# Attention with Toeplitz bias: pieces of the maxima and additions of the outputs on GpSimd, outputs turned later, another order in the last steps

## What is computed

```
proj = layernorm(x) @ w_in.T                     # k, v, q: 16 heads of 8 features
bias[h, i, j] = sum_k amp * exp(-|sharp| * (offset - (i - j))**2)   # depends on i - j: Toeplitz
logits = q @ k.T / sqrt(8) + bias
out = softmax(logits) @ v
x = x + out
```

## Time and profile before

| | |
|---|---|
| profiled execution | 1109.1 us, its span 1107.4 us |
| other runs | 1102.92, 1107.15, 1109.07 us |
| PE busy | 957.4 us (86%) |
| DVE busy | 855.9 us (77%) |
| ACT busy | 677.8 us (61%) |
| POOL busy | 487.8 us (44%) |
| mean granted TensorE clock | 0.934 |

### The profile page before, as it was taken

The page is one execution under the profiler, slowest core; times in us unless marked ns, Lnnn a source line. Parts: engine busy times, 40 slices in busy tenths (PEclk is TensorE's granted clock), DMA queues, the critical chain, the costliest instruction groups (busy, mean ns, idle before and its releaser), DMA issues. The chain is left out here.

```text
span 1107.4 us, 21223 instructions
## 1 busy us (share of the span) xinstructions
PE 957.4 (86%) x7613; PEld 561.8 (51%) x7613; DVE 855.9 (77%) x2203; ACT 677.8 (61%) x1042; POOL 487.8 (44%) x454
## 2 busy tenths in 40 slices
PE   4899999999999999866899999783877359999998
PEld 2423333333333333315777888541666347778886
DVE  7689999999999999766897554586896787975553
ACT  5226665666666566654678888587333136788886
POOL 4400101110110010104689999615674027899997
PEclk9669999999999999998999999996998669999999
DMA  4840223141314310005466677200000045666973
GB/s 103 230 161 17 84 77 72 36 125 39 75 47 113 66 35 2 3 1 145 133 178 175 170 191 193 57 19 1 0 0 0 3 101 156 172 180 159 220 193 95
DMA packets 80613, 105.92 MB, mean 96 GB/s; under 512 B 18252, under 2 KB 41602, under 8 KB 80514
## 3 DMA queue, kind: packets, MB, share of 16 engines
q1 hardware_dynamic: 78631, 102.43, 35.7%
q10 hardware_dynamic: 1883, 2.21, 0.7%
HBM read 95.84 MB, written 8.52 MB: 94 GB/s over the span
## 5 line engine op out<-in xcount | busy, mean ns | idle before, releaser
L663 POOL TENSOR_TENSOR f_act_low<-f_act,f_act_high 128x512 fp32r<-128x512 f32 x272 | 353.1, 1314 | 154.4 <-ACT f_act_high L639 146.6
L1509 DVE CUSTOM_DVE_ANT_0 at_rows<-at_rows,at_table_max 128x512 f32<-128x512 f32 x512 | 340.8, 718 | 26.3 <-PE at_rows L1295 17.0
L1455 ACT ACTIVATE at_prob<-at_cols 128x1024 f32<-128x1024 f32 x256 | 248.1, 1021 | 174.3 <-PE at_cols L1336 174.3
L678 DVE SCALAR_TENSOR_TENSOR f_gated<-f_hid,f_cw 128x512 f32<-128x512 f32 x256 | 174.1, 687 | 115.8 <-ACT f_act L644 86.9
L644 ACT ACTIVATE f_act<-f_gated 128x512 f32<-128x512 f32 x272 | 172.1, 633 | 109.8 <-DVE f_gated L678 78.5
L639 ACT CAST f_act_high<-f_act 128x512 fp32r<-128x512 f32 x272 | 164.9, 607 | 0.0
L1295 PE MATMUL at_rows<-at_k_stack,at_q_stack 48*64 48x512 bf16 x1024 | 128.3, 413 | 16.9 <-DVE at_maxima L1509 15.2
L1348 PE MATMUL at_pv<-at_prob,at_v_stack 128*32 128x512 f32 x1024 | 136.7, 606 | 0.6 <-ACT at_prob L1455 0.6
L1336 PE MATMUL at_cols<-at_table_cols,flip_sum 64*64 64x512 f16 x2048 | 135.4, 380 | 0.0
L610 PE MATMUL f_acc<-f_act_high,wd_high 128*128 128x512 f32 x272 | 109.1, 401 | 9.1 <-POOL f_act_low L663 8.9
L1295 PEld LDWEIGHTS at_rows<-at_k_stack,at_q_stack 48*64 48x64 bf16 x1024 | 36.4, 107 | 146.1 <-DVE at_maxima L1509 124.7
(11 more groups left out here) (322 smaller groups left out, 1360.0 us busy)
## 6 DMA issues: line engine op xcount, KB each, us to landing
f_cw<-f_c_rows SPq DMA_DIRECT2D x256, 256.0 KB, 4.5
at_table_cols<-bias_rows SPq DMA_DIRECT2D x64, 124.0 KB, 4.4
at_table_max<-bias_rows SPq DMA_DIRECT2D x12, 480.0 KB, 4.7
at_q_stack<-q_parts SPq DMA_DIRECT2D x32, 96.0 KB, 2.6
at_k_stack<-k_parts SPq DMA_DIRECT2D x24, 96.0 KB, 3.4
at_raw_weights<-in_L_ffn_up_w_dram SPq DMA_DIRECT2D x8, 256.0 KB, 4.1
at_raw_weights<-in_L_ffn_down_w_dram SPq DMA_DIRECT2D x8, 256.0 KB, 5.7
at_table_max<-bias_rows ACTq DMA_DIRECT2D x4, 480.0 KB, 5.8
```

What stands on the lines that cost most here:

```text
L663: nc.gpsimd.tensor_tensor(act_l[:, n % PART_SLOTS, :], act[:, n % ACT_SLOTS, :], act_h[:, n % PART_SLOTS, :].bitcast(F32), ALU.subtract).t ...
L678: ins = nc.vector.scalar_tensor_tensor(out=gated[:, n % GATE_SLOTS, :], in0=hid[:, n % HID_SLOTS, :], scalar=0.0, in1=cw[:, k % C_SLOTS, u ...
L1455: act(prob[:, S % 2, 2 * hp:2 * hp + 2, :], s2[:, hp, :, :], ACT.Exp).then_inc(exp_done, 1)
L1509: nc.vector.tensor_tensor_reduce(out=slot, in0=slot, in1=t_max[:, 2 * p.hp + j, c:c + BANK][:, ::-1], scale=1.0, scalar=-3.0e38, op0=ALU.a ...
```

## The change

GpSimd cuts the maxima into pieces: VectorE keeps the reduction over the two halves, and four chained GpSimd instructions make the pieces of the positive maximum (`cut_maxima`); the sign moves to the constant, now -1.0. The maxima are double-buffered by phase. GpSimd adds the normalised outputs to x for the first 12 of 16 phases (`add_rows`). In steps S%8 = 2 the outputs are turned behind the first rows pair instead of ahead of it, on TensorE, on VectorE and in the ring's order. The wait for the bias tables stands ahead of the scores. In the steps without rows pairs TensorE's order is scores 0, biases 0, maxima's turn, products of the step before, scores 1, biases 1.

```diff
+ADDED_ON_POOL = PHASES - 2 * BATCH
-TWO_ONES = struct.unpack("<f", struct.pack("<I", 0x3F803F80))[0]
+TWO_MINUS_ONES = struct.unpack("<f", struct.pack("<I", 0xBF80BF80))[0]
+def phase_cut_in(S):
+    n = [n for n in pairs_of_step(S) if n % PHASE_PAIRS == PHASE_PAIRS - 1]
+    return n[0] // PHASE_PAIRS if n else None
...
         for S in range(ALL_STEPS):
             pairs = pairs_of_step(S)
+            for n in pairs[:1]:
+                self.take(("pair", n), 2)
             if phase_out_in(S) is not None:
                 self.take(("out", phase_out_in(S)), 1)
-            for n in pairs[:1]:
-                self.take(("pair", n), 2)
...
-        mx = sb("maxima", [P, MAXIMA, 2])
+        mx = sb("maxima", [P, 2, MAXIMA, 2])
...
+                def cut_maxima(phase):
...
+                    pool.wait_ge(top_ready, phase + 1)
+                    if phase:
+                        pool.wait_ge(fills, slots.end["maxima", phase - 1])
+                    nc.gpsimd.tensor_copy(piece(0), top(0)).then_inc(m_order, 1)
+                    done()
+                    tt(top(1), top(0), piece(0), ALU.subtract).then_inc(m_order, 1)
+                    done()
+                    nc.gpsimd.tensor_copy(piece(1), top(1)).then_inc(m_order, 1)
+                    done()
+                    tt(piece(2), top(1), piece(1), ALU.subtract).then_inc(negm_ready, 1)
+                def add_rows(phase):
...
+                    pool.wait_ge(slots_free, slots.end["out", phase])
+                    tt(rows, rows, onorm[:].rearrange("p t h e -> p t (h e)"), ALU.add).then_inc(x_added, 1)
+
+                cut_maxima(0)
...
+                    if phase_cut_in(S) is not None:
+                        cut_maxima(phase_cut_in(S))
+                    if phase_out_in(S) is not None and phase_out_in(S) < ADDED_ON_POOL:
+                        add_rows(phase_out_in(S))
                     if S - 2 in WEIGHT_STEPS:
                         split_weights(WEIGHT_STEPS.index(S - 2))
...
+                    for n in pairs[:1]:
+                        rows_pair(n)
                     if phase_out_in(S) is not None:
                         turn_outputs(phase_out_in(S))
-                    for n in pairs[:1]:
-                        rows_pair(n)
...
+                    if pairs:
...
+                    else:
+                        scores(S, 0)
+                        biases(S, 0)
+                        if phase_turned_in(S) is not None:
+                            turn_maxima(phase_turned_in(S))
                         products(S - 1)
+                        scores(S, 1)
+                        biases(S, 1)
...
                     if p.last:
-                        negate_maxima(p.phase, slots.end["pair", n])
-
-                def negate_maxima(phase, freed):
...
-                    ch.link(nc.vector.tensor_reduce(mtop[:, 0, :], mx[:], AX_X, ALU.max))
-                    ch.link(ts(piece(0), top(0), -1.0, None, ALU.mult))
-                    ch.link(stt(out=top(1), in0=top(0), scalar=-1.0, in1=piece(0), op0=ALU.mult, op1=ALU.subtract))
-                    ch.link(nc.vector.tensor_copy(piece(1), top(1)))
-                    ch.link(tt(top(2), top(1), piece(1), ALU.subtract))
-                    nc.vector.tensor_copy(piece(2), top(2)).then_inc(negm_ready, 1)
+                        v.wait_ge(slots_free, slots.end["pair", n])
+                        if p.phase:
+                            v.wait_ge(negm_ready, p.phase)
+                        nc.vector.tensor_reduce(mtop[:, 0, :], mx[:, p.phase % 2, :, :], AX_X, ALU.max).then_inc(top_ready, 1)
...
+                    if phase < ADDED_ON_POOL:
+                        return
                     v.wait_ge(slots_free, slots.end["out", phase])
```

More of the change, by code:

```diff
@@ L942, in attention @@
         vst = sb("v_stack", [P, BATCH, LT, G4, 32])
[L943 removed]
+        two_minus_ones, warm = sb("two_minus_ones", [32, P]), sb("warm", [P, 1])
         t_col = sb("table_cols", [P, 2, G4 // 2, COL_W], F16)
@@ L1180, in pool_program @@
                                         channel_multiplier=-1).then_inc(mask_made, 1)
-                nc.gpsimd.memset(two_ones[:], TWO_ONES).then_inc(ones_made, 1)
+                nc.gpsimd.memset(two_minus_ones[:], TWO_MINUS_ONES).then_inc(ones_made, 1)
                 def low_part(n):
@@ L1209, in pool_program, with piece, top, done @@
                 constants_rest(m, pool)
+                def cut_maxima(phase):
+                    def piece(k):
+                        return negm[:, :, k, :]
+                    def top(k):
+                        return mtop[:, k, :].rearrange("p (j n) -> p j n", j=2)
+                    def done():
+                        nonlocal cuts
+                        cuts += 1
+                        pool.wait_ge(m_order, cuts)
+                    pool.wait_ge(top_ready, phase + 1)
[8 more added lines that the diff above has]
+                    tt(piece(2), top(1), piece(1), ALU.subtract).then_inc(negm_ready, 1)
+                cuts = 0
+                def add_rows(phase):
+                    it, lh = phase // 2, phase % 2
+                    c0, t0 = it // BATCH * G4 * HD, it % BATCH * LT + lh * QT
+                    rows = m.x[:, t0:t0 + QT, c0:c0 + G4 * HD]
+                    pool.wait_ge(slots_free, slots.end["out", phase])
+                    tt(rows, rows, onorm[:].rearrange("p t h e -> p t (h e)"), ALU.add).then_inc(x_added, 1)
+                cut_maxima(0)
                 def split_weights(k):
@@ L1384, in tensor_program @@
                                 pe.wait_ge(tab_in[c], 64 * (it // BATCH + 1))
[L1385 to L1389, removed]
+                    if pairs:
+                        for hp in range(2):
+                            scores(S, hp)
+                        if phase_turned_in(S) is not None:
+                            turn_maxima(phase_turned_in(S))
+                        for hp in range(2):
+                            biases(S, hp)
+                        for n in pairs[1:]:
+                            rows_pair(n)
+                        if S > 0:
+                            products(S - 1)
+                    else:
+                        scores(S, 0)
+                        biases(S, 0)
+                        if phase_turned_in(S) is not None:
+                            turn_maxima(phase_turned_in(S))
                         products(S - 1)
+                        scores(S, 1)
+                        biases(S, 1)
                     yield
@@ L1562, in vector_program @@
                     pairs = pairs_of_step(S)
+                    for n in pairs[:1]:
+                        pair_maxima(n)
                     if phase_out_in(S) is not None:
                         add_outputs(phase_out_in(S))
-                    for n in pairs[:1]:
-                        pair_maxima(n)
                     if phase_turned_in(S) is not None:
```

16 lines of the change are left out of this document (3 added, 13 removed).

## The result

In 19 runs of each kernel the changed kernel took 1099.57 us in the median (1094.61 to 1105.65), the kernel before 1106.82; the ratio is 0.9945, interval 0.9927 to 0.9963. That is 6.1 us (4.1 to 8.1) of gain. The forecast gain was 15.7. The time lies inside the range, but less than half of the gain came, 0.55%, and the interval reaches from 0.37 to 0.73%, to both sides of the 0.5% that the prediction's chances go by. One run of the kernel before (1257.75 us), and one in a later comparison (1874.94 us), fell in a slower state and are left out of all ratios. The profiled execution took 1103.92 us around a span of 1102.2.

The account below looks back on a forecast made before the run. The attention's ordinary step was taken as PE-bound, with PE's delays behind DVE as the target. The terms summed to -15.7 us, from the median 1107.15 to 1091.5, stated as 1092; range 1086 to 1102.

Parts of the forecast that it names:

- Maxima cut up on POOL: Attention, steps S%8 = 4: DVE keeps only the reduction; all 14 delays go, POOL's four-instruction chain takes 1.3 us.
- rivals 2 and 3: POOL's chain somewhat late, 1096 to 1097 or 1101 us (chance 0.13); far later, slower than before, 1125 us (0.04).
- Additions on POOL, the slip of 0.2 us: Attention: DVE loses 0.29 us per phase; the 0.2 us slip after outputs goes in 10 phases, 2.0 us.
- Waits and slip: Attention, 76 to 438 us: PE's 17 waits for DVE's maxima go, -18.5, slip -2.0, with +0.25 at step 106.
- Outputs turned behind the first pair: Attention, steps 10 to 106: PE stands still 0.33 us for the slot in each of 13 phases, +4.3 us.
- Last eleven steps: Attention, steps 117 to 127, without rows pairs: period 2.97 us against 2.89, in all +0.95 us.
- Step 122: One of the attention's last eleven steps: -0.15 us in the new order.
- step 118: In the attention's last eleven steps, where exponential and products stop overlapping: +0.4 us once.
- Start: Attention's first 22 pairs, DVE-bound: DVE loses 0.93 us, PE waits for POOL's chain; -0.3 us, from -0.9 to +1.
- The sum of the attention: All attention terms: -18.5 - 2.0 + 0.25 - 0.35 + 4.3 + 0.95 - 0.3 = -15.7 us.
- Rival 4: POOL's added attention instructions hold up DVE's maxima at the shared port; delays stay, about 1107 us; chance 0.08.

Follow-up runs that it names:

- outs_first: Changed kernel with the outputs turned ahead of the first rows pair again; 1099.42 us, ratio 0.9916 to the kernel before.
- last_back: Changed kernel with TensorE's old order in the steps without rows pairs; 1096.40 us, ratio 0.9884 to the kernel before.
- after_ht_first: Changed kernel with GpSimd's wxx waiting also for VectorE's Ht in the state-space loop; 1086.62 us, ratio 0.9832 to the kernel before.

## Why the prediction was wrong

Step by step, as the prediction put them:

- **Maxima cut up on POOL**: right. All 14 delays went; the interval of that step fell from 4.06 to 3.15 us, of which 0.24 is the turn. The chain, taken at 1.3 us with 0.25 each, took 1.05 with 0.20 and 0.22; none of rivals 2 and 3 came up.
- **Additions on POOL, the slip of 0.2 us**: right, the step after the outputs is 2.89 where it was 3.07. Waits and slip together were to give 18.5 + 2.0 - 0.25 = 20.25 us; 19.4 came (steps 8 to 111 take 322.4 instead of 336.5 us, although the outputs' turn costs 5.3 in them).
- **Outputs turned behind the first pair**: right in kind, too small. PE stands from the pair's end (200.03 + 0.24) to 200.69, 0.42 us, not 0.33. DVE's last maximum ended 0.51 us behind the pair's start, as reckoned with 0.52; the hand-over to PE was 0.15 and not 0.05. 13 x 0.41 = 5.3 us for 4.3, and it comes a fourteenth time at step 114. outs_first, with 3.87 instead of 4.28 for this step, shows the 0.41. Not all of it is lost: behind steps 106 and 114 outs_first has a step of 3.97 us where the changed kernel has 2.89, and in all the later turn costs 3.1 us by the two traces.
- **Last eleven steps**: the period is 2.97 as forecast, but the whole is 2.0 us by last_back, not 0.95 (single profiles, whose phases ahead of step 112 are 24.80 us in both). From products to products: seven periods give 0.56. Step 121 is 3.54 us instead of 2.89 (+0.65), as the products wait for ACT's copy; the sum had nothing there. Step 122, put at -0.15, is 3.56 instead of 3.43 (+0.13). At step 118, put at +0.4, nothing is lost (5.23 and 5.22). The products of step 117 come 0.64 earlier in the new order, but the last ones of all come 2.97 us behind those before them where the old order takes 1.68 (+1.29).
- **Start**: -0.3 forecast. Step 0 began at 69.51 us against 69.01, later and not earlier, but step 8 at 95.76 against 96.39. Neither says much, as equal code varies more: step 8 begins at 94.3 to 97.3 us in four profiles with the old attention and at 90.6 to 97.6 in nine with the new one.
- **The sum of the attention**: forecast -15.7, measured -13.4 in the two profiles that are compared. The attention's end scatters with the same code: 489.3 to 494.9 us in those four profiles with the old attention (mean 491.5), 472.8 to 480.0 in those nine with the new one (mean 476.5). By the means it is -15.0, but about 2 of that come ahead of step 8, where -0.3 was forecast. From step 8 on the forecast's terms give -15.35, and the means -13.0 (395.4 and 382.4 us). The mechanisms of this part stood, its size to some 15%; that the whole comes so near is partly luck.
- **The step that failed** is one that the prediction never wrote out: it added the attention's terms and took everything behind the attention to move along unchanged ("from there I get 1091.5"), a term of nothing for which it gave no reason. The loop of the state-space layer gave back 9.1 us (73.3 to 82.4). -15.0 + 9.1 = -5.9, and the ratio says -6.1. Rival 4 named the right port but the wrong stage: it looked for contention among the instructions that were moved, and found rightly that there is none. The loss is in code that the diff doesn't touch, by way of VectorE's instruction count: its loop comes round late, GpSimd gets in first, and PE's longer wait takes the granted clock down in more passes.

The warning was in the trace of before: the same pass, with the same instructions, took 8.3, 8.8 or 10.4 us. The 10.4 is the clock's part, but 8.3 and 8.8 are both at the full clock (Ht takes 0.42 us in the one and 0.91 in the other), and so point to an order that nothing in the program fixes. DVE is busy there for 8.01 of 8.27 us, with POOL at 6.34 beside it. That the loop would tip to the other order could not be had from the trace. That passes could change their length by 0.5 us, and by 2 with the clock, could.

## What to carry to other kernels

Where VectorE and GpSimd both read two SBUF tiles in a loop, look at the passes one by one; if equal passes differ in length at the same granted clock, the order at the shared port may be left to chance, and a wait that fixes the better order (here one wait, 0.6% in the kernel before and 1.1% in the changed one) can be worth as much as many small moves. A change that only takes instructions out of a program can slow down code behind it, so compare the trace stage by stage first, and test a part of a change with the later stages held in the same state. And count what a reordering costs in every step in which it recurs: by the traces, turning the outputs behind the first pair (3.1 us in all) and the new last steps (2.0 us) were both a loss, which the gain of moving the maxima hid.

## What the runs showed of the hardware that I had not expected

- VectorE's loop comes round in 0.46 to 0.57, 0.70 or 0.80 us (last H to next dtx, the same instructions) by its place in the program. The difference lies at the branch back, 0.13 to 0.15 us against 0.26 to 0.31, and goes with an 8192-byte packet on the instruction queue q14 at the loop's start or in its first pass; the reason stays open.
- An order keeps itself up once DVE comes round at the same time in each pass: the kernel before left order B behind its first pass and stayed in A, at 0.46 to 0.60; the changed kernel never left B, at 0.70; and with 2 or 20 memsets one pass was in A and the next fell back.
- The late return and the order cost more by the clock than by themselves: 3.0 us of pass time with the clock up, 6.3 more with passes in which the granted clock is 0.84 instead of 1.00. PE's gap ahead of M's products, in full-clock passes, is 2.66 us in order B, 1.69 or 2.15 in order A, and 1.77 in after_ht_first, where the clock over the loop stays at 0.99.
- Four chained GpSimd instructions on 128x16 take 0.20 to 0.22 us each, with some 0.07 between them.
